# Scan inputs of both halves in one GpSimd instruction, in a fused attention, routed FFN and state-space kernel

## The chip, the cores and the metric

One core of a Trainium2 chip. The metric is the device time of one launch in microseconds; the kernel before has a median of 1981.06 us over 3 runs (1978.12 to 1986.54).

## The reference

Input is `x` of 16 batches x 512 tokens x 256 features, f32. Four layers with a residual around each, and a layer norm (no affine part) in front of each:

```
x = x + attention(layernorm(x))      # RMS norm, 16 heads of 16, causal softmax, Wo, plus its own input
x = x + ffn(layernorm(x))            # base + shared low rank + top 2 of 6 routed low-rank experts
x = x + ssm(layernorm(x))
x = x + ffn(layernorm(x))            # the same weights again
```

The changed part is in `ssm`: a causal convolution of four taps over time and a silu give `xc`; then

```
delta = softplus(xc @ Wd.T + bd);  Bm = xc @ Wb.T;  Cm = xc @ Wc.T      # Bm, Cm: 16 states
for each state n:   h_t = exp(-exp(log_a)[n] * delta_t) * h_(t-1) + delta_t * xc_t * Bm_t[n]
y_t = sum over n of h_t * Cm_t[n];   out = (y * sigmoid(x @ Wg.T + bg)) @ Wo.T + bo
```

## The kernel before, in words

**Stages.** One batch is 512 tokens in four blocks of 128 partitions, or, turned, 256 features in two halves (c = 0, 1) of 128 partitions x 512 tokens. Each batch goes through q and k projections (split in three bf16 parts that are stored in HBM and stacked again by DMA, `stack` L826), scores, exp and product with the values in four groups of four heads, the FFN, the state-space layer with 16 steps n = 0 to 15, one for each state, and the second FFN (the FFN's calls carry a 0 or a 1 in their names). Up to five batches are in flight.

**Order of the work.** No engine loops over batches by itself. Time is cut into ticks `now`; a head group has 20 (`HALF`), a batch 80 (`FRAME`). Tables `PE_AT`, `ACT_AT`, `DVE_AT`, `POOL_AT`, `SP_AT` (L95 to L122) give each call its tick, counted from its batch's start; `OWN` (L123) has other ticks for batch 0 (set 1), batch 14 (set 2) and batch 15 (set 3). Each engine walks over the ticks and issues what is due (`due`, `steps`), so the tables set only the order on each engine's queue; when something runs is set by semaphores. Between these calls VectorE has a "unit" every second tick: `maximum` (L1119), a masked row maximum of one block of scores, 10 units for a head group. `BANK` (L103) says which of two PSUM banks a side matmul fills.

**One step n of the state-space layer.**
- SyncE, `load_b` L850: brings b of step n, repeated over 128 partitions, into `b_all[:, k % 3]`. With three buffers it waits for the inputs of step n - 3. `stack`, `stack_maxima`, `store_parts`, `store` and `load_x` are on the same queue.
- GpSimd, `inputs` L1421: waits for b, for scan n - 2 (two buffers of `inp`) and for its own last call, then multiplies u by b in two instructions of 128x512, c = 0 on L1428 and c = 1 on L1434, with a wait for the first between them. In batch 15 (`s == NB - 1`) GpSimd makes only c = 0; VectorE makes c = 1 from PSUM (`half_of_inputs` L1235).
- ScalarE, `decays` L1012: the exponentials.
- VectorE, `scan` L1242: one tensor_tensor_scan over 128x1024 on L1259, both inputs in SBUF; later `product` L1263 times c of step n, which TensorE has spread over a PSUM bank (`spread_c` L659).
- GpSimd, `add_state` L1437, n from 1, batches 0 to 13: a DMA that adds `hc` into `y` (L1441), after the product and after the add before it has landed. Batches 14 and 15 sum on TensorE instead (`sum_y` L677).

Other calls on GpSimd: `rsqrt` L1399 (4 columns; L1403, L1406, L1408) for each norm, and `weigh_low` L1411 (128x448, L1415). Other VectorE calls with two SBUF inputs: `silu` L1220 and `delta_u` L1226. The two multiplies before:

```
first = G.tensor_tensor(inp[:, n % 2, 0, :], u[:, 0, :], b_all[:, k % 3, :], ALU.mult)
...
    pool.wait_ge(pool_own.sem, pool_own.one())
    G.tensor_tensor(inp[:, n % 2, 1, :], u[:, 1, :], b_all[:, k % 3, :], ALU.mult).then_inc(inp_ready.sem, 1)
```

Of the kernel before, what the change touches and what calls it, by code (L numbers as in the profile page):

```python
# [56 lines left out]
def hybrid_block(nc, x, norm_w, wqk_t, bqk_c, wv_t, bv, wo_t, bo, conv_w, conv_b, wd_t, bd, wbc_t,  # L57
# [37 lines left out]
    PE_AT = {"res": (-31, -30), "xn": (-74, -72), "qk00": (-55, -52, -46), "qk01": (-47, -45, -44),  # L95
# [10 lines left out]
    ACT_AT = {"res": (-32, -29), "square_f": 100, "square_s": 126, "square_l": 252, "norm_f": 103, "norm_s": 129,
# [11 lines left out]
    POOL_AT = {"rsqrt_f": 85, "rsqrt_s": 128, "rsqrt_q": -108, "rsqrt_l": 242, "low": (116, 264),
               "inputs": (146, 149, 154, 156, 162, 164, 167, 174, 198, 201, 203, 213, 214, 215, 218, 223),
               "add": (160, 156, 163, 166, 182, 184, 192, 198, 205, 212, 213, 214, 221, 225, 225, 228)}  # L120
    SP_AT = {"parts": (-43, 6), "load_x": -111, "store_b": 154, "store": 281, "stack": (-28, -29, -30), "maxima": -6,
             "load_b": (154, 160, 160, 168, 168, 169, 177, 183, 189, 198, 204, 205, 214, 222, 223, 224)}  # L122
# [1407 lines left out]
```

## Time and profile before

| | |
|---|---|
| median of 3 runs | 1981.06 us |
| the profiled execution: time, span | 1986.2 us, 1984.4 us |
| TensorE busy, share of span | 1749.4 us, 88% |
| VectorE | 1719.0 us, 87% |
| ScalarE | 1411.7 us, 71% |
| GpSimd | 1182.6 us, 60% |
| granted TensorE clock, mean | 0.963 |
| the page's chain by engine | PE 25%, DMA 21%, DVE 20%, POOL 12%, issue 11%, ACT 9% |

DVE is VectorE, ACT ScalarE, POOL GpSimd, SP SyncE, PE TensorE's matmuls and PEld its weight loads. A group of instructions is shown as line, engine, operation, output<-input with shapes, count, busy time in us and mean ns of one, then the engine's idle time just before them and who ended it. Matmul ends are modelled, so a busy PE is not PE at its peak.

### The profile page before, as it was taken

Reading aid. Unit: us, or ns where it says so; the run is one execution under the profiler, and the core shown is the slowest. Engines: PE = TensorE matmul, PEld = TensorE weight load, DVE = VectorE, ACT = ScalarE, POOL = GpSimd, SP = SyncE. Lnnn points to the kernel's source line nnn. Section 1 sums busy time; section 2 is a strip of 40 time slices with the busy share of each in tenths; the row PEclk is TensorE's granted clock in tenths of the full one; section 3 lists DMA queues with packets and bytes.
Section 4 is the critical chain, followed back from the end, with each engine's and each line's share of the span. In section 5 each row is a group of like instructions: output and inputs, shape, how many; then the busy total and the mean of one; then the engine's idle time right before and its main releaser. Section 6 shows DMA issues by size and latency. Waiting matters only on the chain.

```text
span 1984.4 us, 32798 instructions
## 1 busy us (share of the span) xinstructions
PE 1749.4 (88%) x10311; PEld 1053.3 (53%) x10356; DVE 1719.0 (87%) x3928; ACT 1411.7 (71%) x2724; POOL 1182.6 (60%) x933
## 2 busy tenths in 40 slices
PE   5999788989899898999899898989999898778875
PEld 2555454646465565646465564646565464535333
DVE  5654889998999999899999999899999989977893
ACT  3667668687877868687877868787877868664641
POOL 2001666667767676667767666657667655776530
PEclk9999899999999999999999999999999999998987
DMA  4321676878677786877777776877777777651110
GB/s 139 92 77 48 139 158 142 171 153 173 143 158 168 155 182 145 172 158 166 144 159 170 153 178 148 173 155 163 153 164 162 151 163 146 141 116 54 49 59 11
DMA packets 186094, 275.37 MB, mean 139 GB/s; under 512 B 33809, under 2 KB 125762, under 8 KB 185922
## 3 DMA queue, kind: packets, MB, share of 16 engines
q1 hardware_dynamic: 155682, 163.17, 33.4%
q0 software_dynamic: 30240, 110.11, 29.8%
q8 instruction: 83, 1.36, 0.3%
q14 instruction: 89, 0.73, 0.1%
HBM read 128.49 MB, written 34.08 MB: 82 GB/s over the span
## 4 chain that ended last, share of the span: by engine, by line
PE 25%; DMA 21%; DVE 20%; POOL 12%; issue 11%; ACT 9%; SPq 2%; POOLq 0%; DVEq 0%; ACTq 0%
DMA y<-hc 14%; PE bank L421 7%; DVE hc L1259 6%; DVE bank L1116 5%; POOL inp L1434 4%; POOL inp L1428 4%; PE bank L627 3%; DVE hc L1267 2%; DMA X<-in_x 2%; PE bank L482 2%; DMA sk<-qk_parts 2%; PE bank L504 2%; POOL rs L1406 2%; PE bank L610 2%; PE bank L529 2%
## 5 line engine op out<-in xcount | busy, mean ns | idle before, releaser
L1259 DVE TENSOR_TENSOR_SCAN hc<-dec,inp 128x1024 f32<-128x1024 f32 x256 | 631.3, 2471 | 28.2 <-ACT dec L1017 14.4
L1428 POOL TENSOR_TENSOR inp<-u,b_all 128x512 f32<-128x512 f32 x256 | 428.7, 1675 | 197.1 <-DVE hc L1259 116.8
L1116 DVE CUSTOM_DVE_ANT_0 bank<-bank,mask_qk 128x512 f32<-128x512 f32 (+3 forms) x1024 | 477.9, 508 | 72.2 <-PE bank L482 71.3
L901 ACT ACTIVATE pt<-bank 128x512 f32<-128x512 f32 x640 | 378.0, 596 | 175.9 <-PE bank L506 173.5
L1434 POOL TENSOR_TENSOR inp<-u,b_all 128x512 f32<-128x512 f32 x240 | 409.3, 1705 | 18.8
L1017 ACT ACTIVATE dec<-dt,a_neg 128x511 f32<-128x511 f32 x512 | 339.6, 717 | 48.9 <-DVE hc L1259 48.8
L1441 POOL DMA_DIRECT2D y<-hc x210 | 185.0, 881 | 314.8 <-DMA y<-hc 234.4
L504 PE MATMUL bank<-sq,sk 98*128 98x512 bf16 (+3 forms) x1024 | 275.8, 308 | 44.9 <-ACT pt L901 42.9
L1267 DVE TENSOR_TENSOR hc<-hc,bank 128x1024 f32<-128x1024 f32 x242 | 293.4, 1212 | 19.7 <-PE bank L664 19.1
L482 PE MATMUL bank<-sk,sq 96*128 96x512 bf16 (+3 forms) x1024 | 251.9, 308 | 44.8 <-DVE mall L1116 26.2
L506 PE MATMUL bank<-mask_kq,ident_bf 128*128 128x128 bf16 x1024 | 197.2, 224 | 0.0
L482 PEld LDWEIGHTS bank<-sk,sq 96*128 96x128 bf16 x1024 | 94.4, 99 | 187.2 <-issue 68.0
L529 PE MATMUL bank<-pt,v_sb 128*32 128x512 f32 (+3 forms) x2048 | 179.4, 446 | 1.9 <-ACT pt L901 1.9
L504 PEld LDWEIGHTS bank<-sq,sk 98*128 98x128 bf16 x1024 | 102.4, 100 | 111.1 <-ACT pt L901 54.7
L934 ACT ACTIVATE parts<-bank,bqk 128x512 bf16<-128x512 f32 x192 | 125.5, 686 | 46.1 <-PE bank L421 41.6
L421 PE MATMUL bank<-xt_q,wqk 128*128 128x512 f32 x256 | 142.7, 687 | 1.8 <-ACT xt_q L955 0.7
L1116 DVE DVE_READ_ACCUMULATOR2_ANT mall<- 128x1 f32 x1024 | 142.9, 140 | 0.0
L1406 POOL TENSOR_TENSOR rs<-va,half 128x4 f32<-128x4 f32 x64 | 82.5, 1288 | 90.7 <-DVE ng L1170 86.6
L506 PEld LDWEIGHTS bank<-mask_kq,ident_bf 128*128 128x128 bf16 x1024 | 103.3, 101 | 59.4 <-issue 24.2
L664 PE MATMUL bank<-bcs,onehot 96*128 96x512 bf16 x256 | 99.3, 388 | 38.0 <-DVE hc L1267 36.1
L627 PE MATMUL bank<-xs_t,taps 128*128 128x512 f32 x256 | 116.8, 600 | 0.2
L1415 POOL TENSOR_TENSOR hw<-low,wts 128x448 f32<-128x448 f32 x32 | 65.4, 2044 | 63.4 <-DVE wts L1217 63.4
(167 smaller groups left out, 3118.8 us busy)
## 6 DMA issues: line engine op xcount, KB each, us to landing
y<-hc POOLq DMA_DIRECT2D x210, 512.0 KB, 5.2
b_all<-b_kept SPq DMA_DIRECT2D x256, 256.0 KB, 4.0
qk_parts<-parts SPq DMA_DIRECT2D x96, 256.0 KB, 2.9
sq<-qk_parts SPq DMA_DIRECT2D x384, 64.0 KB, 4.0
sk<-qk_parts SPq DMA_DIRECT2D x384, 64.0 KB, 4.1
X<-in_x SPq DMA_DIRECT2D x16, 512.0 KB, 7.8
out<-X SPq DMA_DIRECT2D x16, 512.0 KB, 4.6
sq<-hlt SPq DMA_DIRECT2D x256, 2.0 KB
```

What stands on the lines that cost most here:

```text
L421: last = mm(dst[:, :], w[:, c, g * P:(g + 1) * P], src[:, c, :], start=(c == 0), stop=(c == C - 1))
L482: return mm(dst[:, o:o + n], sq[0:KS, slot, h, qb * P:(qb + 1) * P], sk[0:KS, slot, h, 0:n], start=True, stop=True)
L504: mm(dst[:, o:o + n], sk[:, slot, h, kb * P:(kb + 1) * P], sq[:, slot, h, kb * P:T], start=True, stop=False)
L506: return mm(dst[:, o:o + P], ident_bf[:, :], mask_kq[:, :], start=False, stop=True)
L529: last = mm(pv_bank[VW * i:VW * (i + 1), kb * P:T], values_of(a, kb, first + i), pt[:, n % PT, at:at + T - kb * P], start=start, stop=stop ...
L901: A(pt[:, n % PT, :], score_bank[unit % 2][:, :], ACT.Exp).then_inc(exp_done.sem, 1)
L1017: last = A(dec[:, n % 2, c, 1:T], dt[:, c, 1:T], ACT.Exp, scale=a_neg[:, c, n:n + 1])
L1116: return V.tensor_tensor_reduce(src[:, o:o + n], src[:, o:o + n], mask_qk[:, T - n:T], 1.0, -3.0e38, ALU.add, ALU.max, out)
L1259: V.tensor_tensor_scan(h, d, v, 0.0, ALU.mult, ALU.add).then_inc(scan_done.sem, 1)
L1267: V.tensor_tensor(hc[:, k % HC, :, :] if n or s >= LATE else y[:, s % 2, :, :], hc[:, k % HC, :, :], spread_bank[:, None, :].to_broadcast( ...
L1428: first = G.tensor_tensor(inp[:, n % 2, 0, :], u[:, 0, :], b_all[:, k % 3, :], ALU.mult)
L1434: G.tensor_tensor(inp[:, n % 2, 1, :], u[:, 1, :], b_all[:, k % 3, :], ALU.mult).then_inc(inp_ready.sem, 1)
```

## The change

`inputs` makes both halves in one instruction where it made two; b is repeated over c by a step of zero. The wait between the halves goes. Batch 15 stays as it was. All tables are new; of `OWN` only the sets' places change, not their meaning. For batches 1 to 13 (the diff shows the tables that the prediction speaks of):

```diff
-                first = G.tensor_tensor(inp[:, n % 2, 0, :], u[:, 0, :], b_all[:, k % 3, :], ALU.mult)
                 if s == NB - 1:
-                    first.then_inc(inp_ready.sem, 1)
+                    G.tensor_tensor(inp[:, n % 2, 0, :], u[:, 0, :], b_all[:, k % 3, :],
+                                    ALU.mult).then_inc(inp_ready.sem, 1)
                 else:
-                    first.then_inc(pool_own.sem, 1)
-                    pool.wait_ge(pool_own.sem, pool_own.one())
-                    G.tensor_tensor(inp[:, n % 2, 1, :], u[:, 1, :], b_all[:, k % 3, :], ALU.mult).then_inc(inp_ready.sem, 1)
+                    G.tensor_tensor(inp[:, n % 2, :, :], u[:, :, :],
+                                    b_all[:, k % 3, None, :].to_broadcast([P, C, T]),
+                                    ALU.mult).then_inc(inp_ready.sem, 1)
...
-    DVE_AT = {"gated": 247, "add_x3": (250, 250), "in0": 112, "in1": 262, "out0": 114, "out1": 271,
-              "add_up1": (277, 277), "add_x1": (94, 94), "add_up0": (125, 125), "silu": 143, "delta": 153,
-              "stats_q": -113, "finish": -9, "heads": 27,
-              "scan": (157, 168, 169, 171, 178, 183, 191, 195, 200, 207, 211, 215, 219, 225, 228, 231),
-              "product": (160, 170, 173, 181, 186, 190, 192, 198, 203, 210, 214, 218, 221, 227, 231, 235)}
-    POOL_AT = {"rsqrt_f": 85, "rsqrt_s": 128, "rsqrt_q": -108, "rsqrt_l": 242, "low": (116, 264),
-               "inputs": (146, 149, 154, 156, 162, 164, 167, 174, 198, 201, 203, 213, 214, 215, 218, 223),
-               "add": (160, 156, 163, 166, 182, 184, 192, 198, 205, 212, 213, 214, 221, 225, 225, 228)}
-    SP_AT = {"parts": (-43, 6), "load_x": -111, "store_b": 154, "store": 281, "stack": (-28, -29, -30), "maxima": -6,
-             "load_b": (154, 160, 160, 168, 168, 169, 177, 183, 189, 198, 204, 205, 214, 222, 223, 224)}
+    DVE_AT = {"gated": 246, "add_x3": (250, 251), "in0": 112, "in1": 263, "out0": 116, "out1": 271,
+              "add_up1": (277, 278), "add_x1": (94, 96), "add_up0": (123, 125), "silu": 141, "delta": 153,
+              "stats_q": -111, "finish": -9, "heads": 26,
+              "scan": (157, 169, 169, 171, 177, 183, 191, 196, 200, 207, 211, 215, 218, 224, 228, 231),
+              "product": (158, 170, 173, 181, 187, 190, 192, 198, 202, 210, 213, 216, 220, 227, 231, 234)}
+    POOL_AT = {"rsqrt_f": 88, "rsqrt_s": 126, "rsqrt_q": -108, "rsqrt_l": 241, "low": (115, 264),
+               "inputs": (146, 149, 152, 156, 162, 164, 173, 180, 197, 199, 202, 214, 215, 216, 218, 223),
+               "add": (160, 156, 162, 170, 180, 185, 193, 197, 204, 212, 214, 215, 222, 223, 224, 227)}
+    SP_AT = {"parts": (-43, 7), "load_x": -112, "store_b": 151, "store": 281, "stack": (-29, -29, -30), "maxima": -5,
+             "load_b": (154, 160, 161, 166, 169, 174, 176, 180, 182, 196, 196, 205, 212, 220, 222, 223)}
```

`PE_AT`, `ACT_AT`, `BANK` and `OWN` change in the same manner, most entries by a tick or two, those of batch 0 by up to 25. Among units a call stands after the unit of its tick, and 80 ticks are one batch, so that ticks 171 and 91 meet; two calls of one batch that stay between the same neighbours keep their order whatever their ticks.

## Rows read from the trace of the kernel before

**Rows 1.** Busy time by stage: PE, PEld, DVE, ACT, POOL, clock, DMA.

```profile
340.00:1574.00 1234.00, 1133.41 (x6985) 694.73 (x7016) 1156.56 (x2661) 965.73 (x1870) 851.41 (x659) 0.98 0.76 161
1793.00:1890.00 97.00, 79.76 (x266) 44.53 (x265) 77.39 (x86) 53.96 (x105) 53.10 (x41) 0.92 0.15 50
```

**Rows 2.** The page, costliest groups: scan and both halves.

```profile
L1259 DVE TENSOR_TENSOR_SCAN hc<-dec,inp 128x1024 f32<-128x1024 f32 x256 | 631.3, 2471 | 28.2 <-ACT dec L1017 14.4
L1428 POOL TENSOR_TENSOR inp<-u,b_all 128x512 f32<-128x512 f32 x256 | 428.7, 1675 | 197.1 <-DVE hc L1259 116.8
...
L1434 POOL TENSOR_TENSOR inp<-u,b_all 128x512 f32<-128x512 f32 x240 | 409.3, 1705 | 18.8
```

**Rows 3.** Waits, 340 to 1574 us: total us, times, longest.

```profile
POOL y L1441 <- DMA y<-hc: 177.6, 69, 7.3
...
PEld bank L482 <- DMA sk<-qk_parts: 19.5, 20, 2.8
...
PE bank L482 <- DMA sk<-qk_parts: 8.6, 11, 1.9
```

**Rows 4.** Single lines, whole run: ns min/median/max.

```profile
L1259 DVE TENSOR_TENSOR_SCAN hc<-dec,inp x256: 2257/2291/4164, 197.4 to 1940.8; 128x1024 f32<-128x1024 f32 x128
...
L1434 POOL TENSOR_TENSOR inp<-u,b_all x240: 1261/1275/3340, 196.1 to 1859.5; 128x512 f32<-128x512 f32 x120
...
L1408 POOL TENSOR_TENSOR nm<-ng,rs x64: 198/202/2092, 8.1 to 1956.6; 128x4 f32<-128x4 f32 x64
...
L1415 POOL TENSOR_TENSOR hw<-low,wts x32: 933/2228/2812, 142.6 to 1969.5; 128x448 f32<-128x448 f32 x32
```

**Rows 5.** Timeline, VectorE, then GpSimd, 901 to 909 us.

```profile
901.90 0.60 DVE L1116 CUSTOM_DVE_ANT_0 bank<-bank,mask_qk 128x384 f32<-128x384 f32 x1
...
902.66 3.28 DVE L1259 TENSOR_TENSOR_SCAN hc<-dec,inp 128x1024 f32<-128x1024 f32 x1
...
901.55 0.92 POOL L1441 DMA_DIRECT2D y<-hc  x1
902.24 1.55 POOL L1428 TENSOR_TENSOR inp<-u,b_all 128x512 f32<-128x512 f32 x1
903.86 3.15 POOL L1434 TENSOR_TENSOR inp<-u,b_all 128x512 f32<-128x512 f32 x1
```

**Rows 6.** Chain of waits, 907 to 919 us.

```profile
907.04 0.32 SPq L857
...
914.33 4.01 DMA sk<-qk_parts
...
918.39 0.39 PE bank L482
```

**Rows 7.** Timeline, VectorE, then GpSimd, 950 to 954 us.

```profile
950.76 4.16 DVE L1259 TENSOR_TENSOR_SCAN hc<-dec,inp 128x1024 f32<-128x1024 f32 x1
...
951.20 1.57 POOL L1428 TENSOR_TENSOR inp<-u,b_all 128x512 f32<-128x512 f32 x1
952.84 3.15 POOL L1434 TENSOR_TENSOR inp<-u,b_all 128x512 f32<-128x512 f32 x1
```

**Rows 8.** Timeline, VectorE, then GpSimd, 726 to 728 us.

```profile
726.51 2.29 DVE L1259 TENSOR_TENSOR_SCAN hc<-dec,inp 128x1024 f32<-128x1024 f32 x1
...
727.05 2.82 POOL L1428 TENSOR_TENSOR inp<-u,b_all 128x512 f32<-128x512 f32 x1
```

**Rows 9.** Timeline, VectorE, then GpSimd, 963 to 970 us.

```profile
966.17 0.69 DVE L1116 CUSTOM_DVE_ANT_0 bank<-bank,mask_qk 128x512 f32<-128x512 f32 x1
...
966.78 1.22 DVE L1223 SCALAR_TENSOR_TENSOR xc<-sp_t,xc 128x1024 f32<-128x1024 f32 x1
...
968.64 2.63 DVE L1259 TENSOR_TENSOR_SCAN hc<-dec,inp 128x1024 f32<-128x1024 f32 x1
...
963.40 2.09 POOL L1428 TENSOR_TENSOR inp<-u,b_all 128x512 f32<-128x512 f32 x1
...
967.01 2.12 POOL L1428 TENSOR_TENSOR inp<-u,b_all 128x512 f32<-128x512 f32 x1 [0.17 <-POOL inp L1434]
```

More of the change, by code:

```diff
@@ L138, in hybrid_block @@
-            "DVE": {"in0": 111, "in1": 265, "out1": 268, "add_x1": (89, 90), "add_up0": (118, 121), "silu": 142,
-                   "scan": (155, 167, 169, 173, 179, 180, 190, 193, 202, 205, 211, 215, 217, 224, 225, 232),
-                   "product": (165, 171, 171, 177, 182, 188, 193, 198, 204, 206, 211, 216, 219, 229, 231, 235)},
-            "POOL": {"rsqrt_f": 92, "rsqrt_s": 123, "rsqrt_q": -118, "rsqrt_l": 239, "low": (117, 263),
-                   "inputs": (140, 146, 146, 147, 155, 160, 171, 173, 196, 201, 203, 210, 214, 219, 219, 221),
-                   "add": (160, 152, 156, 165, 173, 175, 175, 196, 203, 210, 213, 215, 219, 221, 222, 226)},
@@ new lines, in hybrid_block @@
+            "ACT": {"res": (-31, -45), "square_f": 92, "square_s": 125, "square_l": 251, "norm_f": 100,
[4 rows of a table added]
+                   "decays": (154, 164, 167, 170, 171, 180, 185, 188, 199, 203, 203, 208, 214, 215, 223, 226)},
+            "DVE": {"gated": 244, "add_x3": (250, 250), "in0": 111, "out0": 111, "out1": 269, "add_up1": (276, 278),
+                   "add_x1": (90, 91), "add_up0": (119, 125), "delta": 152, "stats_q": -108,
+                   "scan": (157, 166, 171, 171, 180, 180, 187, 190, 203, 208, 210, 211, 220, 225, 226, 230),
+                   "product": (166, 170, 175, 179, 185, 189, 192, 200, 204, 209, 210, 217, 221, 227, 231, 233)},
@@ new lines, in hybrid_block @@
+            "POOL": {"rsqrt_s": 127, "rsqrt_q": -112, "rsqrt_l": 237, "low": (113, 263),
+                   "inputs": (145, 147, 147, 148, 158, 164, 174, 182, 197, 200, 201, 206, 214, 218, 218, 221),
+                   "add": (160, 148, 162, 170, 174, 183, 183, 200, 203, 211, 213, 216, 219, 220, 225, 226)},
+            "SP": {"parts": (-33, -6), "load_x": -117, "store_b": 145, "store": 279,
+                   "load_b": (151, 156, 156, 162, 169, 179, 183, 183, 189, 193, 202, 208, 209, 212, 216, 225)},
+        },
[8 rows of a table added]
+                   "sum": (168, 171, 178, 181, 188, 199, 204, 206, 208, 213, 219, 227, 232, 234, 239, 242)},
+            "ACT": {"res": (-37, -31), "square_f": 99, "square_l": 245, "norm_q": -102, "exp1": 262,
[4 rows of a table added]
+                   "decays": (154, 154, 166, 170, 173, 176, 193, 193, 198, 206, 210, 215, 216, 224, 225, 230)},
+            "DVE": {"gated": 234, "add_x3": (251, 250), "in0": 113, "in1": 265, "out0": 115, "out1": 266,
+                   "add_up1": (286, 287), "add_x1": (93, 94), "add_up0": (125, 125), "silu": 140, "delta": 154,
+                   "scan": (156, 168, 170, 174, 174, 181, 191, 195, 198, 205, 210, 212, 217, 222, 222, 229),
+                   "product": (164, 169, 173, 180, 182, 187, 192, 197, 204, 206, 211, 219, 219, 223, 224, 230)},
+            "POOL": {"rsqrt_f": 86, "rsqrt_s": 130, "rsqrt_l": 247, "low": (110, 264),
+                   "inputs": (146, 149, 150, 150, 153, 168, 176, 178, 196, 198, 199, 211, 214, 214, 216, 229),
+                   "add": (160, 152, 158, 163, 182, 194, 207, 208, 210, 215, 215, 217, 223, 225, 225, 230)},
+            "SP": {"parts": (-45, 6), "load_x": -111, "store_b": 150, "store": 302,
+                   "load_b": (159, 159, 166, 168, 180, 184, 184, 187, 188, 189, 202, 207, 210, 216, 221, 224)},
+        },
[8 rows of a table added]
+                   "sum": (172, 172, 176, 189, 190, 192, 197, 202, 205, 209, 220, 221, 227, 231, 233, 241)},
+            "ACT": {"res": (-31, -29), "square_s": 129, "square_l": 248, "norm_f": 107, "norm_s": 131,
[5 rows of a table added]
+                   "decays": (158, 160, 163, 165, 165, 171, 186, 187, 199, 201, 201, 207, 213, 219, 227, 236)},
+            "DVE": {"gated": 242, "add_x3": (248, 249), "in0": 114, "in1": 262, "out0": 115, "out1": 272,
+                   "add_up1": (275, 276), "add_x1": (94, 98), "add_up0": (119, 121), "silu": 142, "delta": 152,
+                   "stats_q": -113,
+                   "scan": (162, 162, 171, 175, 182, 183, 193, 197, 199, 207, 211, 213, 222, 224, 229, 236),
+                   "product": (168, 169, 173, 176, 182, 190, 194, 197, 205, 207, 212, 216, 222, 226, 229, 240)},
+            "POOL": {"rsqrt_f": 92, "rsqrt_s": 120, "rsqrt_q": -114, "rsqrt_l": 238, "low": (116, 276),
+                   "inputs": (151, 151, 151, 161, 170, 171, 177, 183, 202, 205, 211, 214, 217, 218, 218, 229),
+                   "add": (160, 162, 174, 178, 185, 188, 190, 197, 197, 203, 209, 213, 231, 236, 239, 247)},
+            "SP": {"parts": (-40, 4), "load_x": -111, "store": 298,
+                   "load_b": (152, 156, 163, 165, 167, 181, 181, 184, 190, 198, 201, 206, 210, 210, 221, 225)},
```

45 lines of the change are left out of this document (8 added, 37 removed), and 88 rows, old and new, of tables (ACT_AT, OWN, PE_AT).

## The prediction

> **What bounds the kernel now.** I read the stages first, then the waits, then single instructions around the changed lines. In the steady stage (some eleven of sixteen batches, 340 to 1574 us) VectorE is busy 1156.6 of 1234 us, 94%, and TensorE 1133.4, 92%, while GpSimd has 851.4, 69% [rows 1]. A batch takes 1234 / 11 = 112 us there, and VectorE has some 7 us of idle in it. So a microsecond more or less on VectorE counts nearly whole, one on GpSimd counts only if somebody waits for it. Who does: TensorE's score matmuls wait 19.5 + 8.6 = 28.1 us in 31 places for the stacked q and k [rows 3], whose DMAs stand on SyncE's queue behind loads of b that wait for the scan inputs. GpSimd's longest wait, 177.6 us, is for its own adds into y to land [rows 3]; a faster multiply doesn't shorten that.
>
> The groups show what the change touches: 256 first halves at 1675 ns, 240 second halves at 1705 ns, 256 scans at 2471 ns [rows 2]. The spread matters more. A second half has a median of 1275 ns and a longest of 3340; a scan a median of 2291 and a longest of 4164 [rows 4]. Mean less median, times the count, is 0.43 x 240 = 103 us for the second halves and 0.18 x 256 = 46 us for the scans. The two engines wait for each other. At 902 us that is seen singly: the first half runs from 902.24 until 903.79, the scan arrives at 902.66 and takes 3.28 us, 1.0 over its median, so it only began when that half was done; the second half, issued at 903.86, takes 3.15 us and ends a half's time after the scan [rows 5]. The gap between the halves lets the scan in. A blocked second half is 3.15 - 1.275 = 1.87 us longer; 103 / 1.87 makes some 55 such places in the run, about four in each steady batch.
>
> The Trainium skill (SBUF — State Buffer, section "Who interferes with whom") states it as an exclusive lock: a VectorE instruction with two SBUF inputs and a GpSimd one that reads SBUF exclude each other for the whole instruction, and issue order decides who waits. The rows at 902 us agree; by that rule this change doubles the longest hold, and speaks against it. What it would do here is my forecast's third term, worked out from rows.
>
> **The change part by part.**
> *The instruction.* Two of 128x512 and a wait become one of 128x1024. Undisturbed, two halves take 2 x 1.275 = 2.55 us and the 0.07 us between them, 2.62. The new shape isn't in the trace. Bounds: 128x4 takes 0.202 us and 128x512 1.275 [rows 4], so a column costs 1.073 / 508 = 2.1 ns and 1024 take 0.202 + 1020 x 0.0021 = 2.35 us. The other end is the nearest instruction with a repeated operand, 128x448 with a median of 2.23 us, least 0.93 [rows 4]: at 5 ns a column it would be 5.1 us, though most of that median is blocked time. I take 2.35, 0.27 saved a step. The Trainium skill (GPSIMD Engine Reference, section 3.1) gives 4497 ns for 2048 columns; a line from 1.275 us to that would give about 2.35 too, an estimate by that page. Of 240 steps the saving counts only where the scan is waiting for it: step 12 and step 0 of a batch. 2 x 14 x 0.26 = **-7 us** (bounds 0 and 240 x 0.27 = -65).
>
> *SyncE.* load_b of step n + 3 waits for the inputs of step n, and the stack of the next head group is behind it. The inputs of step 5 end at 907.01 because a scan blocked them; SyncE's load goes out at 907.04, the last part of sk lands at 918.34 and a score matmul begins at once [rows 6]. In one piece they end 0.26 (step 4's saving in front of them) and then 2.1 us sooner, at about 904.6. The waits for sk are 31 in eleven batches, some three a batch of 0.9 us; I take one away: 13 x -0.9 = **-12 us** (bounds 0 and -2.6 x 13 = -33). By the due times the order load_b 8, stack, maxima stays.
>
> *VectorE.* In batches 1 to 13 GpSimd's calls keep their order, but for one of batch 14 that comes sooner; only the due times change. VectorE's order changes by a maximum unit here and there. I walk the four collisions of a steady batch:
> - Step 4. The scan now stands one unit earlier (product 2, unit, add, unit, add, scan). The unit is 902.66 - 901.90 = 0.76 us [rows 5], so the scan arrives at 901.90. Step 5's inputs follow an add's DMA issue and would be issued at 902.24 - 0.26 = 901.98. Is 0.08 us enough to be first? At 950.76 a scan was 0.44 us ahead of the inputs and still lost (4.16 us long) [rows 7]; at 726.51 one was 0.54 ahead and won [rows 8]. So it loses, and waits for 1.08 us more (2.35 - 1.27): the inputs end at 904.6, the scan at 906.8, and with the unit now behind it VectorE is at 907.5 where it was at 905.9: +1.6.
> - Step 10: same calls in the same order, race lost as before, the hold is 1.08 longer: +1.1.
> - Step 13. silu, two SBUF inputs, moves a unit earlier, to 966.17; step 13's inputs, issued at 963.40 [rows 9], now hold until about 966.6. silu then ends at 967.7, step 14's inputs hold until 970.0, and the scan, due at 969.1, ends at 972.2 instead of 968.64 + 2.63 = 971.3: +0.9.
> - Step 14: its 0.07 us of blocking goes: -0.1.
> Together +3.5 us a batch, 13 x 3.5 = 45 us. VectorE's 7 us of idle a batch takes up some; I count two thirds, **+30 us** (bounds: every stall of a scan gone, -46; all 55 places 1.08 us longer and nothing absorbed, +59).
>
> *Batch 0, batches 14 and 15, and all other new places.* Batch 15 keeps its half on VectorE. The last stages are loose (VectorE 77.4 of 97 us [rows 1]), and there the chain goes by TensorE and the scans. Orders change for a few calls; I have no row with a sign: 0, bounds -10 and +10. The banks, the same number of fills in two banks, cost nothing as TensorE's waits for a free bank are under those for data.
>
> Sum: -7 - 12 + 30 = **+11 us** on the profiled execution's 1986.2. That one is 5.1 us over the runs' median of 1981.06, so against the median I say **1992 us**. About 0.5% (10 us) is what a measurement can tell from no change, so this is just over it.
>
> **Rivals.**
> *A, faster: the scan gets in first.* Place: step 4's scan against step 5's inputs. It decides at some 0.5 us of lead [rows 7, 8]; any call that is late on GpSimd, an add that waits for its DMA above all, gives that lead. Then step 4 saves its 1.0 us stall in place of +1.6, and step 10's collision may go too (-1.87 instead of +1.1), since everything behind it moves. VectorE then has 3.5 - 2.6 = +0.9 or, with step 10, -2.1 a batch: +12 to -27, by two thirds +8 to -18; with GpSimd's -19 that is -11 to -37, so 1944 to 1970, I say 1966. For it: GpSimd is free earlier at every step, so its adds and waits shift. Against: by the rows both races are lost.
> *B, no change.* The halves' saving and the longer hold meet, or both vanish in the 31% of GpSimd's time that is free and the 6% of VectorE's: 1981, say 1972 to 1991. For it: orders hardly differ in the steady stage. Against: VectorE is at 94%.
> *C, much slower: the wide instruction is slow.* If the repeated b costs what the 128x448 form's median says, an instruction takes 4 us or more, 240 x 1.4 = 336 us on GpSimd, 69% becomes 86%, and each hold grows by 1.4 us again: 55 x 1.4 x 2/3 = +51 on top, about 2043. Against: the repeat is over whole rows of 512, not inside a row of 16.
>
> **How the numbers follow.** My case, the longer hold: 0.37, own range 1983 to 2015. A 0.33, B 0.26, C 0.04. Slower by over 0.5% is my case and C, 0.41; faster is A, 0.33; same B, 0.26. Cases of both signs hold most, so the range reaches across: 1960 leaves a tenth below, in A; 2014 leaves a tenth above, C and my case with more new collisions.
>
> **What would show it.** Right: the new group near 2.35 us by its shortest and not far over it by its mean (few are blocked half way, so mean less median shrinks); the scan's mean up from 2471 ns to about 2640 (45 us over 256 more), its longest near 5.2 us (4.16 + 1.08); step 4 and step 10 scans long in most batches; waits for sk below 28 us in the steady stage; a batch of 112.9 us instead of 112.2. Wrong: a scan's mean at or under 2471 with a shorter batch says A; a shortest instruction over 2.6 us says C; a scan that is longer with a batch that isn't says that VectorE has more room than I gave it.

## The result, and the profile after

The changed kernel takes 2004.6 us (median of 4 runs, 1987.6 to 2008.5) against 1979.6 beside it: a ratio of 1.0105, 95% interval 1.0063 to 1.0148. It is slower by about 1%. The profiled execution has 2004.75 us and a span of 2003.0, 18.6 us more than the 1984.4 of before.

The page after: busy time by engine, the chain by engine, and the two groups that answer to [rows 2]. Lines behind the tables are three further on.

```profile
PE 1754.9 (88%) x10311; PEld 1053.5 (53%) x10356; DVE 1749.1 (87%) x3928; ACT 1404.1 (70%) x2724; POOL 1029.8 (51%) x693
...
PE 39%; DVE 21%; DMA 13%; issue 11%; ACT 9%; POOL 4%; SPq 2%; POOLq 0%; DVEq 0%; ACTq 0%
...
L1435 POOL TENSOR_TENSOR inp<-u,b_all 128x1024 f32<-128x1024 f32 x240 | 677.5, 2823 | 221.2 <-DVE hc L1262 133.4
L1262 DVE TENSOR_TENSOR_SCAN hc<-dec,inp 128x1024 f32<-128x1024 f32 x256 | 645.5, 2528 | 28.8 <-ACT dec L1020 12.6
```

GpSimd is busy 1029.8 us where it had 1182.6. It was freed of 153 us, and the kernel became slower. VectorE is busy 30 us more, half of it in the scans: (2528 - 2471) x 256 = 14.6 us. The steady stage and its waits, for [rows 1] and [rows 3]:

```profile
340.00:1574.00 1234.00, 1125.51 (x6891) 685.63 (x6922) 1162.76 (x2628) 946.50 (x1844) 720.77 (x477) 0.98 0.75 159
```

```profile
POOL y L1444 <- DMA y<-hc: 161.8, 77, 6.2
...
PEld bank L485 <- DMA sk<-qk_parts: 9.4, 11, 1.7
...
PE bank L485 <- DMA sk<-qk_parts: 1.6, 4, 0.8
```

The same 1234 us hold 6891 matmuls where they held 6985: 1.3% less work done. The waits for the stacked q and k fell from 28.1 us to 11.0. Single lines over the whole run, shortest, median and longest in ns, for [rows 4] (the last two are VectorE's silu and the small subtraction in the router of the FFN):

```profile
L1435 POOL TENSOR_TENSOR inp<-u,b_all x240: 2338/2636/4369, 199.2 to 1877.4; 128x1024 f32<-128x1024 f32 x120
...
L1262 DVE TENSOR_TENSOR_SCAN hc<-dec,inp x256: 2259/2290/5247, 201.7 to 1959.6; 128x1024 f32<-128x1024 f32 x128
...
L1411 POOL TENSOR_TENSOR nm<-ng,rs x64: 198/202/2286, 8.2 to 1975.4; 128x4 f32<-128x4 f32 x64
...
L1226 DVE SCALAR_TENSOR_TENSOR xc<-sp_t,xc x16: 1218/1598/3257, 179.5 to 1872.0; 128x1024 f32<-128x1024 f32 x16
...
L1196 DVE TENSOR_TENSOR lg<-low,red x32: 182/182/2932, 141.1 to 1985.7; 128x24 f32<-128x24 f32 x32
```

The instruction costs 2.338 us at least, nothing unusual. So the loss has to be looked for batch by batch. I took the start of each batch's scan 4 from the timeline and the distance to the next batch's, in us, from batch 1 on:

```
before    112.4 112.7 112.3 109.8 114.3 112.5 110.0 112.5 113.4 110.1 114.2 112.7 | 106.0  97.3
after     119.7 108.8 108.1 108.5 108.8 108.8 111.0 120.7 110.6 117.7 125.9 116.2 | 113.1  95.8
```

**That is the result in one view.** Before, a batch takes 112.2 us in the mean; the three short ones (batches 4, 7 and 10, 109.8 to 110.1) are those in which scan 10 takes 2.29 us, and in the eight in which it takes 4.16 the mean is 113.0. After, there are undisturbed batches of 108.6, which are 3.6 us *faster* than that mean of 112.2, and disturbed ones of 110 to 126. Over the twelve up to the bar the first kind would give 12 x -3.6 = -43 us, the disturbances add 61, and the sum is the +17.9 us by which this stretch is longer (1364.8 against 1346.9). The start up to batch 1's scan 4 is 4.6 us shorter, the end behind batch 13's 5.2 longer: which makes up the span's 18.6, rounding aside.

What a disturbance is shows in the timeline. First batch 7, where these scans are not held, scans 10 and 11 on VectorE and what GpSimd issues between (start us, us; an idle time stands in brackets):

```profile
1044.11 1.22 DVE L1270 TENSOR_TENSOR hc<-hc,bank 128x1024 f32<-128x1024 f32 x1
...
1045.86 2.29 DVE L1262 TENSOR_TENSOR_SCAN hc<-dec,inp 128x1024 f32<-128x1024 f32 x1
...
1051.29 2.29 DVE L1262 TENSOR_TENSOR_SCAN hc<-dec,inp 128x1024 f32<-128x1024 f32 x1 [0.63 <-ACT dec L1020]
...
1047.88 0.92 POOL L1444 DMA_DIRECT2D y<-hc  x1 [2.98 <-issue]
1048.57 2.63 POOL L1435 TENSOR_TENSOR inp<-u,b_all 128x1024 f32<-128x1024 f32 x1
```

Then the same place in batch 8, the same calls in the same order:

```profile
1160.53 1.22 DVE L1270 TENSOR_TENSOR hc<-hc,bank 128x1024 f32<-128x1024 f32 x1
...
1162.28 5.25 DVE L1262 TENSOR_TENSOR_SCAN hc<-dec,inp 128x1024 f32<-128x1024 f32 x1
...
1168.04 1.21 DVE L1270 TENSOR_TENSOR hc<-hc,bank 128x1024 f32<-128x1024 f32 x1
...
1169.90 5.08 DVE L1262 TENSOR_TENSOR_SCAN hc<-dec,inp 128x1024 f32<-128x1024 f32 x1
...
1162.05 0.92 POOL L1444 DMA_DIRECT2D y<-hc  x1 [0.72 <-DVE hc L1270]
1162.72 2.65 POOL L1435 TENSOR_TENSOR inp<-u,b_all 128x1024 f32<-128x1024 f32 x1
1169.55 0.87 POOL L1444 DMA_DIRECT2D y<-hc  x1 [4.18 <-DVE hc L1270]
1170.17 2.65 POOL L1435 TENSOR_TENSOR inp<-u,b_all 128x1024 f32<-128x1024 f32 x1
```

Scan 10 stands 0.53 us behind product 9 in both. The difference is add 9, which waits for product 9 and for add 8's landing. In batches 1 to 7 and 9, add 8 landed at or after product 9's end (6.9 to 8.7 us behind scan 9's start, product 9 ending at 6.84), and the wait kept GpSimd back until the scan had begun. In batches 8 and 10 it had landed at 5.26 and 5.73: add 9 goes out 0.30 us behind the product and inputs 11 0.67 behind that, 0.44 us after the scan's recorded start, and the scan loses. Then there is **a chain**: the late scan 10 is followed by unit, product 10, unit, scan 11, and product 10 releases add 10 and with it inputs 12 just before scan 11, which loses 2.8 us too; then scan 12. Long scans of 5.06 to 5.25 us stand at steps 10, 11 and 12 of batches 8, 10 and 11, at 11 and 12 of batch 12, at 8 of batches 8 and 13, and at 10 of 13: 14 of them, and step 4 was lost in batches 1, 11 and 13 besides. There the router's subtraction `lg` runs into a GpSimd instruction too and takes 2.93 us instead of 0.18, so that in batch 1 scan 5 starts 5.0 us late; where the rest of that batch's 11 us comes from is open.

A wait for a landing can also come out too long. Batch 7 takes 111.0 us although it loses none of these races: its add 9 goes out 1.92 us behind add 8's landing (usual is some 0.5) and lands after 7.1 us, so add 10 and inputs 12 are late, and scan 12 finds VectorE idle:

```profile
1056.17 2.63 POOL L1435 TENSOR_TENSOR inp<-u,b_all 128x1024 f32<-128x1024 f32 x1
...
1058.89 2.29 DVE L1262 TENSOR_TENSOR_SCAN hc<-dec,inp 128x1024 f32<-128x1024 f32 x1 [2.77 <-issue]
```

Batch 9 (110.6 us) has 1.49 us of it at the same scan. What made the adds late is open.

Batch 8 shows one more kind of disturbance, called the second mechanism below. In batch 7 GpSimd's four-column multiply `nm` (of `rsqrt` in front of the FFN) slips in 0.20 us ahead of scan 5, and ScalarE normalises at once:

```profile
1005.45 2.29 DVE L1262 TENSOR_TENSOR_SCAN hc<-dec,inp 128x1024 f32<-128x1024 f32 x1
...
1005.25 0.20 POOL L1411 TENSOR_TENSOR nm<-ng,rs 128x4 f32<-128x4 f32 x1
...
1005.48 2.08 ACT L914 ACTIVATE tok_f<-X,nm,rs 128x256 f32<-128x256 f32 x4 [0.39 <-POOL nm L1411]
```

In batch 8 both start at 1116.10; the multiply is held for the whole scan, ScalarE for 2.67 us, and the score matmuls and VectorE's maxima behind it for 0.93 + 1.83:

```profile
1116.10 2.29 DVE L1262 TENSOR_TENSOR_SCAN hc<-dec,inp 128x1024 f32<-128x1024 f32 x1
...
1122.43 0.57 DVE L1119 CUSTOM_DVE_ANT_0 bank<-bank,mask_qk 128x384 f32<-128x384 f32 x1 [0.93 <-PE bank L485]
...
1125.13 0.43 DVE L1119 CUSTOM_DVE_ANT_0 bank<-bank,mask_qk 128x256 f32<-128x256 f32 x1 [1.83 <-PE bank L485]
...
1116.10 2.29 POOL L1411 TENSOR_TENSOR nm<-ng,rs 128x4 f32<-128x4 f32 x1
...
1118.42 2.08 ACT L914 ACTIVATE tok_f<-X,nm,rs 128x256 f32<-128x256 f32 x4 [2.67 <-POOL nm L1411]
```

### The profile page after: what moved, and what is told of

It reads as the page before. It is cut to its first block, busy times and chain, and to the rows that moved or that the text cites. A ratio compares the mean times of both kernels' runs of the same rounds, so it can differ in the third digit from the quotient of the medians.

```text
span 2003.0 us, 32557 instructions
## 1 busy us (share of the span) xinstructions
PE 1754.9 (88%) x10311; PEld 1053.5 (53%) x10356; DVE 1749.1 (87%) x3928; ACT 1404.1 (70%) x2724; POOL 1029.8 (51%) x693
## 4 chain that ended last, share of the span: by engine, by line
PE 39%; DVE 21%; DMA 13%; issue 11%; ACT 9%; POOL 4%; SPq 2%; POOLq 0%; DVEq 0%; ACTq 0%
DMA y<-hc 11%; PE bank L424 7%; DVE hc L1262 7%; DVE bank L1119 5%; PE bank L532 3%; PE bank L485 3%; PE bank L613 3%; PE bank L630 3%; PE bank L507 3%; PE bank L434 3%; DVE hc L1270 3%; POOL inp L1435 2%; PE bank L614 2%; PE bank L418 2%; DMA sk<-qk_parts 1%
## 5 line engine op out<-in xcount | busy, mean ns | idle before, releaser
L1435 POOL TENSOR_TENSOR inp<-u,b_all 128x1024 f32<-128x1024 f32 x240 | 677.5, 2823 | 221.2 <-DVE hc L1262 133.4
L1262 DVE TENSOR_TENSOR_SCAN hc<-dec,inp 128x1024 f32<-128x1024 f32 x256 | 645.5, 2528 | 28.8 <-ACT dec L1020 12.6
L630 PE MATMUL bank<-xs_t,taps 128*128 128x512 f32 x256 | 122.1, 622 | 0.1
L1409 POOL TENSOR_TENSOR rs<-va,half 128x4 f32<-128x4 f32 x64 | 66.0, 1031 | 92.2 <-DVE ng L1173 88.1
L1186 DVE SCALAR_TENSOR_TENSOR X<-bank,X 128x256 f32<-128x256 f32 x192 | 72.8, 418 | 35.0 <-PE bank L614 23.4
```

The lines of the kernel that those rows point to most:

```text
L1262: V.tensor_tensor_scan(h, d, v, 0.0, ALU.mult, ALU.add).then_inc(scan_done.sem, 1)
L1435: G.tensor_tensor(inp[:, n % 2, :, :], u[:, :, :], b_all[:, k % 3, None, :].to_broadcast([P, C, T]), ALU.mult).then_inc(inp_ready.sem, 1)
```

## The experiments

Each ratio is against the kernel before, measured beside it, with its 95% interval. Four questions: what the instruction and what the tables do (1, 2, 8), what happens when the scans can't lose (3, 4, 5), when the chain alone is broken (6, 7, 9), and whether `nm` is what is left (10, 11, 12).

### 1 and 2. Instruction and tables apart

The first has the new tables and the two old halves, the second the old tables and the one instruction:

```diff
 # e1: the kernel after, but
-                    G.tensor_tensor(inp[:, n % 2, :, :], u[:, :, :], b_all[:, k % 3, None, :].to_broadcast([P, C, T]), ALU.mult)...
+                    first.then_inc(pool_own.sem, 1)
+                    pool.wait_ge(pool_own.sem, pool_own.one())
+                    G.tensor_tensor(inp[:, n % 2, 1, :], u[:, 1, :], b_all[:, k % 3, :], ALU.mult)...
 # e2: the kernel before with the opposite edit
```

> The changed kernel's tables with the two instructions of before. Theory (lost races): in the changed kernel 12 of 13 dense places that cost over 2.5 us come from GpSimd's instruction being issued within 0.5 us of a scan, and a blocked scan then lasts 5.1 to 5.2 us. With halves the same races are lost, but each costs 1.9 us and not 2.9: longest scan 4.2 us, and the time falls by about 1 us a lost place plus what they set off, to 1975 to 1990. Rival (the new tables are to blame, by their order on the queues): the time stays at 2000 or over. Rival (evenly longer hold, as the prediction had it): about 1985, with stalls at the same steps in every batch.

> The kernel before with the one instruction of 128x1024 and the tables of before. Theory (lost races): steps 4 and 10 lose their race as before, each costs 1.08 us more (scans of 4.4 and 5.2 us), step 13 too: some 3 us a batch, 2000 to 2020. Rival (the new tables are to blame): 1970 to 1982, since GpSimd has 150 us less to do and nothing else is changed.

| | two halves | one instruction |
|---|---|---|
| old tables | 1 | 2052.4 us, 1.0366 (1.0341 to 1.0390) |
| new tables | 2016.1 us, 1.0180 (1.0145 to 1.0215) | 2004.6 us, 1.0105 (1.0063 to 1.0148) |

The instruction alone costs 3.7%, some 72 us; the new tables take 48 of them back, but with two halves they are worse than the old. Both expectations were missed; the first kernel came out where its rival that blames the tables had it (2000 or over), the second above every range. In the second kernel the scans add 42 us, as the lines show, and two other VectorE instructions with two SBUF inputs add 53 together (silu 23.7 us before, 44.6 here; the small subtraction 6.5 before, 38.3 here):

```profile
L1259 DVE TENSOR_TENSOR_SCAN hc<-dec,inp x256: 2257/2286/5256, 198.7 to 2012.6; 128x1024 f32<-128x1024 f32 x128
...
L1193 DVE TENSOR_TENSOR lg<-low,red x32: 182/184/2972, 139.1 to 2038.5; 128x24 f32<-128x24 f32 x32
...
L1223 DVE SCALAR_TENSOR_TENSOR xc<-sp_t,xc x16: 1220/3158/3412, 177.1 to 1924.3; 128x1024 f32<-128x1024 f32 x16
```

Here step 4's scan is long (4.1 to 4.6 us) in eleven batches and step 10's (5.24) in ten of 1 to 13, as I had forecast for the kernel after; scans 11 and 12 aren't long in the steady batches, since in the old tables no unit stands between product 10 and scan 11. In the first kernel the scans are no worse than before by their mean (2458 ns), but the chain is there: scans 10, 11 and 12 take 4.0 to 4.2 us in batches 4, 5, 8 and 11. So the chain comes with the new tables, not with the one instruction, which only makes it longer. And the batches without a long scan 10, 11 or 12 take 112 to 115.5 us too: `nm` starts 0.05 to 0.22 us behind scan 5 in eleven batches and is held for over 2 us. That was the first sight of the second mechanism.

### 3 and 4. All lost races taken away

At the steps where a scan had been long, inputs n wait for scan n - 1 where they waited for scan n - 2; kernel after (3) and before (4):

```diff
-                pool.wait_ge(scan_done.sem, scan_done.at(s, n - 1))
+                pool.wait_ge(scan_done.sem, scan_done.at(s, n if n in (5, 9, 11, 12, 13, 14) else n - 1))
```

> The changed kernel, with the inputs of steps 5, 9, 11, 12, 13 and 14 held back until the scan of the step before has ended (they wait for one scan more), so that they can't be issued ahead of it. Theory (lost races): every batch is like its undisturbed ones, which take 108 to 109 us from step 4 to step 4 where before took 112.2; no scan over 3.1 us in the steady stage; 1940 to 1955, under both kernels. Rival (evenly longer hold costs 0.7 of VectorE's stall): 2004 less 55 x 1.1, also under before, but with batches of 110. Rival (holding back makes the inputs late, scans wait for them): scans sit idle for POOL and the time stays at 1990 or over.

> The kernel before (two halves, its tables), with the same steps held back by one scan. Theory (lost races): the stalls of steps 4 (1.0 us), 10 (1.9) and 13 (0.35) go, 3.2 us in each of 13 batches: 1940 to 1955, so before itself was paying for a lost race. Rival (VectorE has room for it, PE sets the pace): within 8 us of 1980.

Measured 2023.5 us, 1.0218 (1.0188 to 1.0248), and 2017.3 us, 1.0188 (1.0139 to 1.0236). Missed by 69 and 62 us. Hardly a scan of steps 4 to 13 is long in batches 1 to 12, but the collision moved: inputs 15, not held, come up just ahead of scan 14, which takes 4.84 us (4.05 with halves) in twelve batches. And `nm` starts 0.04 us (0.53 with halves) behind scan 5 in most batches and takes 2.25 us (1.75). Most batches take 112 to 114 us in both, and in the third run batch 1's scan 4 starts 19 us later than in the kernel after (355.3 us against 336.5). A hold is itself a delay on GpSimd, and shifts what comes behind.

### 5. Without the hold of step 14

```diff
-                pool.wait_ge(scan_done.sem, scan_done.at(s, n if n in (5, 9, 11, 12, 13, 14) else n - 1))
+                pool.wait_ge(scan_done.sem, scan_done.at(s, n if n in (5, 9, 11, 12, 13) else n - 1))
```

> The changed kernel with the inputs of steps 5, 9, 11, 12 and 13 held back until the scan of the step before has ended; step 14 is free again, which in the run that also held step 14 let the inputs of step 15 run ahead of scan 14 (4.84 us in twelve batches). Theory (a race that the landing of the add before decides): in an undisturbed batch of the changed kernel these five start behind that scan anyway, so nothing changes there, and the chain of lost races in steps 8 to 12 can't start: all batches 108 to 111 us, 1945 to 1965. Rival (anything held back shifts everything behind it): batches of 112 to 113 as in the run that held six, 2005 or over.

Measured 2005.1 us, 1.0105 (1.0061 to 1.0149). The forecast was missed; it is the rival's range (2005 or over, batches of 112 to 113). In the steady batches now only scan 13 is long (3.07 us): the excess of all scans over 2.291 us is 16.9 us where the kernel after has 61.7. Yet the time is the same. The start up to batch 1's scan 4 is 16 us longer (352.8 us against 336.5), and the twelve batches behind it are only 11 us shorter (1353.8 against 1364.8). The eight distances from batch 2 on are 111.3 to 114.3 us, and `nm` is held in ten of batches 2 to 12:

```profile
1032.58 2.29 DVE L1262 TENSOR_TENSOR_SCAN hc<-dec,inp 128x1024 f32<-128x1024 f32 x1
...
1032.61 2.25 POOL L1411 TENSOR_TENSOR nm<-ng,rs 128x4 f32<-128x4 f32 x1
...
1034.90 2.07 ACT L914 ACTIVATE tok_f<-X,nm,rs 128x256 f32<-128x256 f32 x4 [2.68 <-POOL nm L1411]
```

So the sum of the scans' stalls doesn't set the time: 45 us of them went, and these batches take 112.5 us where the undisturbed ones of the kernel after take 108.6. Whether the ten holds of an instruction of 0.2 us do that is what experiment 11 asks.

### 6 and 7. Inputs ahead of the adds

Inputs 11, 12 and 13 are issued ahead of adds 9, 10 and 11, so that no add releases them beside a scan; kernel after (6) and before (7):

```diff
-               "inputs": (146, 149, 152, 156, 162, 164, 173, 180, 197, 199, 202, 214, 215, 216, 218, 223),
+               "inputs": (146, 149, 152, 156, 162, 164, 173, 180, 197, 199, 202, 212, 214, 215, 218, 223),
 # in the kernel before
-               "inputs": (146, 149, 154, 156, 162, 164, 167, 174, 198, 201, 203, 213, 214, 215, 218, 223),
+               "inputs": (146, 149, 154, 156, 162, 164, 167, 174, 198, 201, 203, 212, 213, 214, 218, 223),
```

> The changed kernel with the inputs of steps 11, 12 and 13 set ahead of the adds of steps 9, 10 and 11 on GpSimd's queue in batches 1 to 13. They are then not released by the product that also releases scan n + 1, but start when the scan two steps before them ends, 3 us or more ahead of the next scan. Theory (race): scans 10, 11 and 12 stay at 2.3 us, batches 108 to 110 us, 1945 to 1970. Rival (the adds are delayed and scans wait for the hc buffer): no long scans, but idle time of scans behind DMA y<-hc, 1990 or over.

> The kernel before, two halves, with the same three inputs set ahead of the same three adds. Theory (race): scan 10 falls from 4.16 to 2.3 us in the ten batches where it was long, 1.9 us each, and no new long scans: 1955 to 1970. Rival (VectorE has room for a stall of that size): 1975 to 1985.

Measured 1979.6 us, 0.9975 (0.9949 to 1.0000), and 1978.0 us, 0.9974 (0.9955 to 0.9993). The first is right in its mechanism: the chain is gone from the steady batches and 25 us with it. It missed the expected range by 10 us. What its trace shows in place of the lost scans is that the inputs, now further ahead, meet other instructions of VectorE; that this is the whole of the 10 us wasn't tested.

```profile
1052.03 2.23 DVE L1143 TENSOR_SCALAR hl<-mall 128x16 bf16<-128x16 f32 x1
...
1051.87 2.36 POOL L1435 TENSOR_TENSOR inp<-u,b_all 128x1024 f32<-128x1024 f32 x1 [0.17 <-POOL nm L1411]
```

This one, 16 columns with one SBUF input, takes 0.17 us elsewhere; its 64 take 32.0 us together instead of some 11, and the 16 of silu 41.4 instead of 27.1. The second missed its forecast too and lies in the range of its rival (VectorE has room for a stall of that size). In the kernel before, the same edit ended scan 10's stall of 1.87 us (nine batches had it; three now have one of 0.75) and put 0.21 us on scans 11 and 12 of most batches: the scans have 10.5 us less in all, of which 1 to 9 by the interval reach the time. But VectorE's busy time did not fall (1724.6 us against 1719.0): silu and the second of the two small instructions that write `hl` take 17 us more. So the run doesn't tell room from stalls that moved.

### 8. One instruction only where nothing meets it

Kernel before, with the one instruction except at the steps whose inputs a scan had met:

```diff
+                if s < NB - 1 and n not in (5, 9, 11, 13, 14, 15):
+                    G.tensor_tensor(inp[:, n % 2, :, :], u[:, :, :], b_all[:, k % 3, None, :].to_broadcast([P, C, T]), ALU.mult)...
+                    return
```

> The kernel before with its tables; one instruction of 128x1024 in steps 0 to 4, 6, 7, 8, 10 and 12, two halves in steps 5, 9, 11, 13, 14 and 15, those that met a scan. Theory (the wide instruction costs only where a scan meets it): long scans as before, GpSimd about 90 us less busy, 1970 to 1985. Rival (the wide instruction costs by itself, wherever it stands): a good part of the 72 us that it cost everywhere, 2005 to 2035.

Measured 1976.6 us, 0.9975 (0.9952 to 0.9997), as expected, and the long scans are those of before; but GpSimd is only 31 us less busy (1151.1 against 1182.6), not 90. 150 of 240 steps have the one instruction under the old tables and cost nothing; all 240 cost 72 us. The price of the instruction lies in the steps where something stands beside it.

### 9. The chain alone

The kernel after, with two holds only:

```diff
-                pool.wait_ge(scan_done.sem, scan_done.at(s, n - 1))
+                pool.wait_ge(scan_done.sem, scan_done.at(s, n if n in (11, 12) else n - 1))
```

> The changed kernel with the inputs of steps 11 and 12 alone held back until the scan of the step before has ended. The runs that held step 5 too had no chain of lost races and were still at 112 to 113 us a batch; in them the four-column multiply nm of rsqrt for the FFN is issued 0.03 us after scan 5 and is blocked 2.25 us in 11 or 12 batches, where the changed kernel has it 0.20 us ahead and unblocked. Theory (two races: inputs against scans 10 and 11, nm against scan 5): here nm is ahead again, and the chain doesn't start: most batches 108 to 110, 1950 to 1965. Rival (nm is an accident, batches without a chain need 112 as held kernels show): 1995 to 2005.

Measured 1970.4 us, 0.9936 (0.9916 to 0.9957): 5 us over the expected range, and 25 under the rival's. **Two waits on GpSimd take 34 us from the changed kernel**, and it is now faster than the one before. The eight distances from batch 2 on are 107.9 to 109.4 us; `nm` isn't held in any of batches 2 to 12 (in batch 8 it starts 0.02 us ahead of the scan and passes). The four batches of the chain (8, 10, 11 and 12) take 448.4 us together where they took 480.5: 32 us. In batch 8 its lost scan 8 and the held `nm` are gone with it, so that this batch's 12 us aren't the chain's alone. Step 4 is still lost in batches 1, 11 and 13; batches 1 and 11 take 115.5 and 115.8 us.

### 10. `nm` made late in the kernel before

```diff
+                if kind == KIND_F:
+                    for j in range(3):
+                        G.memset(pad[:, 4 * j:4 * j + 4], 0.0)
```

(`pad` is a tile that nothing reads.)

> The kernel before with three memsets of 128x4 on GpSimd between the power and the multiply nm of rsqrt for the FFN after attention, some 0.3 us in each of 16 batches, on an engine that is busy 60%. They write a spare tile; the output is unchanged. Theory (nm against scan 5): nm, now 0.17 us ahead of scan 5, comes behind it and waits 2.1 us, ScalarE with it: 3 to 4 us in each of some 12 batches, 2015 to 2030. Rival (0.3 us on a free engine is nothing, at worst its own length): 1978 to 1986.

Measured 1979.7 us, 0.9991 (0.9975 to 1.0007), in the rival's range. But this didn't test the theory: the three moved `nm` by 0.12 us only, from 0.17 ahead of scan 5 to 0.05, and it still passed. What it gives is the place of the edge: in batches 1 to 13 of all kernels, `nm` passes when its recorded start is 0.02 us or more ahead of scan 5's, and is held from 0.00 on.

### 11. Scan 5 waits for `nm`

Experiment 5 with one wait more, on VectorE, the engine with the least room:

```diff
+                if n == 5 and 1 <= s <= 12:
+                    dve.wait_ge(scaled[KIND_F].sem, scaled[KIND_F].at(s + 1))
```

> The run that held five steps (2005 us), with one more wait: in batches 1 to 12 scan 5 waits until nm of the next batch is done. Theory: scan 5 starts 0.25 us later, nm isn't blocked, ScalarE gets it 2 us sooner, and the batch falls from 112.4 to 109: 1955 to 1970; a wait added on VectorE makes the kernel some 40 us faster. Rival (the held steps cost, not nm): 2005 or over.

Measured 1968.6 us, 0.9924 (0.9903 to 0.9946), as expected. The scan gives way by 0.20 us, and 36 us go by the medians (28 of them in the twelve batches behind batch 1's scan 4 of the profiled executions, 1325.6 us against 1353.8):

```profile
1014.87 2.29 DVE L1264 TENSOR_TENSOR_SCAN hc<-dec,inp 128x1024 f32<-128x1024 f32 x1 [0.20 <-POOL nm L1413]
...
1014.63 0.20 POOL L1413 TENSOR_TENSOR nm<-ng,rs 128x4 f32<-128x4 f32 x1
...
1014.87 2.08 ACT L914 ACTIVATE tok_f<-X,nm,rs 128x256 f32<-128x256 f32 x4 [0.63 <-POOL nm L1413]
```

The eight distances from batch 2 on are 109.0 to 109.5 us where experiment 5 has 111.3 to 114.3. With the same holds in both, this shows the second mechanism and its price: some 3 us a batch.

### 12. The holds from batch 2 on

In experiment 11 the first distance, from batch 0's scan 4 to batch 1's, is 123.3 us, against 111.4 in experiment 9 (the next ones are 111.9 and 115.5). So batches 0 and 1 get the two holds of 9, the later ones those of 11:

```diff
-                if n == 5 and 1 <= s <= 12:
+                if n == 5 and 2 <= s <= 12:
...
-                pool.wait_ge(scan_done.sem, scan_done.at(s, n if n in (5, 9, 11, 12, 13) else n - 1))
+                pool.wait_ge(scan_done.sem, scan_done.at(s, n if n in ((5, 9, 11, 12, 13) if s > 1 else (11, 12)) else n - 1))
```

> The run in which scan 5 waits for nm and five steps are held (1968.6 us), but batches 0 and 1 have only steps 11 and 12 held and no wait for nm. From batch 3 on that run has batches of 109.0 to 109.5 us; scan 4 of batch 2 starts at 474 us, where the run with two held steps has 454. Theory (races): the steady batches stay at 109 and the 20 us at the start come back: 1948 to 1960, under before by more than 1%. Rival (the late start is caught up later anyway, so it costs nothing): 1965 to 1970.

Measured 1962.2 us (1957.8 to 1965.6), 0.9905 (0.9878 to 0.9931); the forecast missed by 2 us. It was built on a misreading: the 474 and 454 us in it are the start of batch 1's scan 4 with the distance from batch 0 added once more (350.9 + 123.3 and 342.7 + 111.4), while batch 2's scan 4 starts at 462.8 and 458.2, so that the 20 us to be had were 5. It beats both kernels, the changed one by 42 us. The first distance is 110.6 us again and the next 117.4, so batch 2's scan 4 stands at 456.7 us where experiment 11 had 462.8: the 6 us gained. The others are 109 to 110 us, but for 113.0 in batch 4 and 111 to 114 from batch 10 on. What makes batch 1 long, with step 4 lost there in this run as in 9, is not settled by it.

## Why the prediction was right, and where it wasn't

The side was right, and 2004.6 lies in 1960 to 2014. Against the runs beside it the change is +25 us where I had forecast +11. But the sum came near for partly wrong reasons, and that it did is in good part luck: races that I had as lost were won, and others that I had no term for were lost.

- **The instruction: right.** Shortest 2.338 us, taken 2.35. Its mean of 2.823 is further over that than I meant by "not far": those that start beside a scan are held, the longest at 4.369, since a scan that wins is itself in the way.
- **SyncE and the stacks: right by its row.** 28.1 us of waits became 11.0, that is 17 where I counted 12 over a slightly longer stretch. What it is worth in the time wasn't tested by itself.
- **VectorE, +30: the term that failed.** It stood for 45 us more of busy time, 3.5 in every batch, most of it from two lost races (steps 4 and 10). The busy time rose by 30.1, and from elsewhere: the scans 14.6 in the net of races lost and won, the subtraction `lg` 9.7 (6.5 to 16.2), silu 3.4. The size for one lost race was right: step 10 went from 4.16 to 5.25 us, +1.09 for 1.08. Its count wasn't. I wrote "Step 10: same calls in the same order, race lost as before". It was lost in 4 of 13 batches, where before it had been lost in 9. The calls beside the race were the same, but a norm's statistics (`stats_q` in the diff, 2 us on VectorE) moved from ahead of scan 9 to behind it: product 9 ends 6.84 us after the scan's start in batches 1 to 10, instead of 4.88 in batches 1 to 9 before. Against scan 9's start, add 8 goes out some 4 us ahead in the kernel before and 0 to 2.5 after; there it lands at 5.3 to 8.7 around the product's end at 6.84, where it landed at 2.9 to 4.7, ahead of the end at 4.88. Before, two of the four batches in which scan 10 won (10 and 12) had such a late landing too, at 9.8 and 7.2 us. So in nearly every batch the wait for that landing decides, not the order (batch 7 before is the exception: add 9 goes out at 6.57 us, though add 8 had landed at 2.95). The row that I had for it (177.6 us of waiting for landings [rows 3]) I took as something that the change doesn't touch, and of VectorE's order I had said that "a maximum unit here and there" moves.
- **Step 4: rival A was true of it.** I moved the scan by one unit and left GpSimd where it was, which gave a lead of 0.08 us. The lead was 0.55 in the undisturbed batches, and it won there, by the very bound of some 0.5 us that [rows 7, 8] gave:

```profile
999.21 2.29 DVE L1262 TENSOR_TENSOR_SCAN hc<-dec,inp 128x1024 f32<-128x1024 f32 x1
...
996.39 0.20 POOL L1411 TENSOR_TENSOR nm<-ng,rs 128x4 f32<-128x4 f32 x1
996.76 2.37 POOL L1435 TENSOR_TENSOR inp<-u,b_all 128x1024 f32<-128x1024 f32 x1 [0.17 <-POOL nm L1411]
999.08 0.91 POOL L1444 DMA_DIRECT2D y<-hc  x1
999.76 3.90 POOL L1435 TENSOR_TENSOR inp<-u,b_all 128x1024 f32<-128x1024 f32 x1
```

  The missing 0.47 stands a call earlier. A norm's `rsqrt` goes ahead of step 4's inputs and waits for ScalarE; against the scan its first instruction starts 1.95 us later (4.20 ahead in place of 6.15), 0.76 of it the scan's own move, and is 0.72 shorter (0.19 in place of 0.91, no longer held by scan 3): +0.47. In batches 1, 11 and 13 the inputs start 0.18 behind, 0.42 ahead and 0.43 behind, and the scan loses.
- **Steps 4 and 10 won** go far to explain the 3.6 us by which an undisturbed batch is faster than the mean before. The batches in which scan 10 had won before took 110.0; of the 1.4 us from there to 108.6, step 4's stall is 1.0. Neither was tested by itself, and experiment 7, which took scan 10's stall away, gained less.
- **What I had no term for.** The chain: a lost scan 10 makes 11 and 12 lose 2.8 us each, since the product that releases the next inputs stands a unit ahead of the next scan. I called step 10's price +1.1; a chain's is 2.96 + 2 x 2.8 = 8.5, and experiment 9 shows that breaking it is worth some 34 us, batch 8's `nm` and scan 8 included. `nm`: I had its longest of 2092 ns in [rows 4] and gave it no price, nor one to the small VectorE instructions. And I took a steady batch to be like every other; but the mean of 112.2 us already hid batches of 110.0 and 113.0 before, by scan 10 won or lost, which would have shown that this race goes both ways.
- **Step 13** took 3.07 us where I had 3.1 (969.1 to 972.2), in eight batches; silu's lines sum to 3.4 us more, where I had some 0.9 a batch.
- **The signs that I named** turned out mixed: a scan's mean of 2528 ns, between the 2471 that would say A and my 2640, is this mixture. The sentence that a longer scan with a batch that isn't longer says "more room" was too simple: experiment 5 has shorter scans than before (a mean of 2353 ns) and takes 1% more time.
- **Rival A, 1966 us at 0.33,** wasn't far off in kind: with the chain broken the changed kernel takes 1970.4 us (experiment 9).

What isn't shown: what tips batches 8 and 10 while 7 and 9 pass. In batch 8 the held `nm` comes first and then a lost scan 8, and in experiment 9 batch 8 is at the edge of it (0.02 us); for batch 10 I have no cause. The spread of the changed kernel's runs (1987.6 to 2008.5) would fit one or two chains more or less, which is argued only.

## What to carry to other kernels

When two engines exclude each other on SBUF, as GpSimd and VectorE do in the holds shown here, a longer instruction costs nothing where nothing meets it (150 steps here) and lengthens the hold where something does (scan 10: 4.16 to 5.25 us); so it is the lost races that must be counted, one by one, with the lead of each, and the lead is set by what the later engine waits for, a DMA's landing included, not by the order of the calls. Look at the repeated unit of work singly: the mean of 113.7 us after the change is made of 108.6 and up to 126, that of 112.2 before of 110 and 113, and the gain to be had (1.7% from the changed kernel by two waits, some 2% by the last form) lay between them. A hold put in to win a race moves everything behind it and can lose another (experiments 3 to 5), so each has to be read again in its own trace. A wait that lets a short instruction past, put on the busiest engine, can be the cheapest change of all: 0.2 us that saved 3 a batch.

## What the runs showed of the hardware

- A 128x1024 multiply on GpSimd with b repeated by a step of zero takes 2.34 us at its shortest, where the line through 128x4 and 128x512 without a repeat gives 2.35 ([rows 4]): nothing is paid for the repeat.
- Who wins isn't told by the recorded starts alone. Close behind a DMA issue of GpSimd, inputs that start 0.44 us *after* a scan's recorded start win (scans of 5.25 us), and lose at 0.47 to 0.55; [rows 7, 8] and the two kernels keep to these bounds. It is not a sharp edge: in experiments 1 and 2 scans 8 win with leads of 0.26 to 0.43 us (seven places, 2.29 us long), and in experiment 10 one loses with 0.47. Where the issue had ended a microsecond or more before, a scan wins with 0.22. But `nm`, behind another GpSimd multiply, loses when it starts at the scan's recorded start and wins at 0.02 ahead. I have no cause for the difference.
- The issue of an add (0.9 us on GpSimd) doesn't hold a scan: the one at 999.21 overlaps it by 0.78 us and takes 2.29.
- The smallest instructions are held as long as the widest: 0.20 us became 2.29 on GpSimd, 0.18 became 2.93 on VectorE (`lg`, two SBUF inputs). A `TENSOR_SCALAR` of 16 columns from f32 to bf16, one SBUF input, was held to 2.23. The Trainium skill (SBUF — State Buffer, section "Who interferes with whom") lists `tensor_scalar` among those that can take the shared ports by themselves; the trace agrees, down to 16 columns.
